# One mask and a tie count in place of sixteen strikes, with the next tile's maxima between dependent steps

## The reference

```python
q = (x @ Wq.T).reshape(b, n, 2, HEADS, DIM_KEY).transpose(2, 0, 1, 3, 4)
sim = jnp.einsum('pbnhd,hkpd->pbnhk', q, keys)
sx, ix = jax.lax.top_k(sim[0], 16)
sy, iy = jax.lax.top_k(sim[1], 16)
all_scores = (sx[..., :, None] + sy[..., None, :]).reshape(b, n, HEADS, 256)
scores, pk_indices = jax.lax.top_k(all_scores, 16)
h = gelu(einsum('bnd,bnhkd->bnhk', x, W_down[pk_indices]))
out = einsum('bnhk,bnhkd->bnd', h * softmax(scores), W_up[pk_indices])
```

## Time and profile before

| | us |
|---|---|
| median of 3 runs | 284.59 (283.16 to 284.63) |
| profiled execution | 284.64 |
| its span, first to last instruction | 282.8 |
| VectorE busy | 269.3 (95%) |
| TensorE busy | 242.3 (86%) |
| ScalarE busy | 236.1 (83%) |
| GpSimd busy | 224.1 (79%) |

### The profile page before, as it was taken

One profiled execution on the slowest core, in us unless ns is written; L12 is line 12 of the kernel. 1 busy time (PEld: TensorE's weight loads), 2 busy tenths in 40 slices (PEclk: granted clock), 3 DMA queues, 4 the chain that ended last, 5 costly groups with the idle time before them and its releaser, 6 DMA issues.

```text
span 282.8 us, 7961 instructions
## 1 busy us (share of the span) xinstructions
PE 242.3 (86%) x1574; PEld 176.7 (62%) x1574; DVE 269.3 (95%) x2580; ACT 236.1 (83%) x1047; POOL 224.1 (79%) x342
## 2 busy tenths in 40 slices
PE   7899797887988798989898889888888888889991
PEld 7566243575866675766576657666666666667780
DVE  5799999979999999999999999999999999999885
ACT  2465768589898999899989999999999999996943
POOL 7888610388688879997999799988998899888852
PEclk9999999797999999999999999999999999999997
DMA  7920000000000000100010001000010001000102
GB/s 174 279 71 2 0 1 0 2 1 0 5 1 0 5 0 3 39 1 3 1 38 3 1 0 38 7 0 5 10 31 2 0 1 41 2 1 3 37 3 74
DMA packets 11235, 6.29 MB, mean 22 GB/s; under 512 B 1457, under 2 KB 10674, under 8 KB 11186
## 3 DMA queue, kind: packets, MB, share of 16 engines
q1 hardware_dynamic: 9858, 5.12, 6.8%
q10 hardware_dynamic: 1328, 0.66, 1.1%
HBM read 3.67 MB, written 2.10 MB: 20 GB/s over the span
## 4 chain that ended last, share of the span: by engine, by line
DVE 62%; PE 14%; issue 8%; POOL 7%; ACT 6%; DMA 2%; ACTq 0%; POOLq 0%; DVEq 0%
DVE rest L1141 24%; DVE top L1130 13%; DVE top L1150 13%; DVE last L1174 6%; PE s_bank L1493 2%; DMA fwq_sb<-in_L_ffn_Wq 2%; POOL squareT L493 2%; DVE slot_gap L1159 2%; PE sim L1507 2%; PE f_bank L1500 1%; PE t_bank L1456 1%; PE c_bank L1500 1%; PE scratch L1487 1%; PE t_bank L1525 1%; POOL wgt L506 1%
## 5 line engine op out<-in xcount | busy, mean ns | idle before, releaser
L1141 DVE MATCH_REPLACE8 rest<-top,sim 128x32 f32<-128x32 f32 x512 | 85.8, 179 | 0.1
L1150 DVE MAX8 top<-rest 128x8 f32<-128x32 f32 x512 | 53.5, 177 | 0.7
L821 ACT ACTIVATE prob<-drop 128x50 f32<-128x50 f32 x224 | 51.6, 256 | 0.0
L1130 DVE MAX8 top<-sim 128x8 f32<-128x32 f32 x496 | 50.9, 178 | 0.6 <-PE sim L1507 0.6
L821 ACT ACTIVATION_READ_ACCUMULATOR prob<-drop 128x1 f32 x224 | 47.1, 214 | 0.0
L493 POOL TENSOR_TENSOR squareT<-sideT 100x512 bf16<-100x512 bf16 x31 | 32.5, 1048 | 15.2 <-ACT sideT L735 15.2
L1141 DVE MATCH_VALUE_LOAD rest<-top,sim 128x8 f32 x512 | 40.8, 80 | 0.3
L478 POOL TENSOR_TENSOR past<-gap,last 128x400 f32<-128x400 f32 x31 | 26.8, 864 | 11.2 <-DVE last L1174 11.2
L1507 PE MATMUL sim<-sim_w,xT_all 128*128 128x512 f32 x64 | 34.5, 621 | 0.8 <-ACT xT_all L771 0.8
L506 POOL TENSOR_TENSOR wgt<-prob,rden 128x400 f32<-128x400 f32 x30 | 25.6, 855 | 8.2 <-DVE rden L1120 8.2
L500 POOL TENSOR_TENSOR drop<-gap,out_by 128x400 f32<-128x400 f32 x30 | 31.0, 1034 | 0.9 <-ACT out_by L724 0.9
(11 more groups left out here) (289 smaller groups left out, 724.0 us busy)
## 6 DMA issues: line engine op xcount, KB each, us to landing
out<-y_sb SPq DMA_DIRECT2D x7, 256.0 KB, 2.3
x_sb<-in_L_attn_hidden_states SPq DMA_DIRECT2D x2, 256.0 KB, 4.0
fwq_sb<-in_L_ffn_Wq ACTq DMA_DIRECT2D x2, 256.0 KB, 6.0
x_sb<-in_L_attn_hidden_states SPq DMA_DIRECT2D x1, 512.0 KB, 5.4
wc_sb<-in_L_attn_Wc SPq DMA_DIRECT2D x1, 256.0 KB
out<-last_y SPq DMA_DIRECT2D x2, 128.0 KB, 1.9
wo_in<-in_L_attn_Wo SPq DMA_DIRECT2D x1, 192.0 KB
keys_sb<-in_L_ffn_keys ACTq DMA_DIRECT2D x1, 128.0 KB, 3.4
```

What stands on the lines that cost most here:

```text
L821: last = nc.scalar.activation(prob[d][:, h, :], drop[:, h, :], ACT.Exp, scale=-1.0, accum_out=den[d][:, h:h + 1])
L1130: last = nc.vector.max(top[d][:, v, 0:8], sim_bank[d][:, bass.ts(v, KEYS)])
L1141: last = nc.vector.match_replace(out=rest[:, v, :], in_to_replace=top[d][:, v, 0:8], in_values=sim_bank[d][:, bass.ts(v, KEYS)], imm_value ...
L1150: last = nc.vector.max(top[n % 2][:, v, 8:16], rest[:, v, :])
```

## The change

The strikes go. The eighth maximum of each vector becomes a threshold: one instruction marks all scores at or over it (`mark_above`, 16 x 32 elements, bf16 out), one adds the mark times -1e38 to the scores (`strike_above`). If scores equal to the eighth were struck too many, they have to come back: `sum_above` counts the marks of each vector into the freed bank, `spill_above` and `put_ties` turn a count over eight into copies of the eighth value in eight further columns of `rest` (now 40 wide), from which `next_8` takes its maxima. Each step needs the one before.

The order changes with it. In a turn, the `first_8` of the next tile stands in two halves between these steps, and the next tile's mark before `next_8`; `maxima` comes after `put_ties`. `top` has three buffers instead of two. `sim_used` is counted once a tile. TensorE computes the scores of tile n+2 late in turn n, not those of n+1 in the middle, and in the prelude the scores of tiles 2 to 5 stand earlier. The four `first_turn` calls are written out as `first_turns`, and the gaps of tile 1 are taken inside `select_tokens`. Lines of the same kind are left out where "..." stands.

```diff
+STRUCK = -1e38
+SPILL = 1e37
+TIES = VECS
-        top = [sb(f"top{i}", [P, VECS, TOPK]) for i in range(2)]
-        rest = sb("rest", [P, VECS, KEYS])
+        top = [sb(f"top{i}", [P, VECS, TOPK]) for i in range(3)]
+        above = sb("above", [P, VECS, KEYS], BF16)
+        rest = sb("rest", [P, VECS, KEYS + 8])
...
-            def strike_8(n, q):
...
-                for v in range(q * VECS // 4, (q + 1) * VECS // 4):
-                    last = nc.vector.match_replace(out=rest[:, v, :], in_to_replace=top[d][:, v, 0:8],
-                                                   in_values=sim_bank[d][:, bass.ts(v, KEYS)],
-                                                   imm_value=NO_SCORE)
+            def first_8(n, halves=range(2)):
+                if n >= 3:
+                    dve.wait_ge(topT_ready, n - 2)
+                dve.wait_ge(sim_ready, n + 1)
+                for v in range(HALF_V * halves[0], HALF_V * (halves[-1] + 1)):
+                    last = nc.vector.max(top[n % 3][:, v, 0:8], sim_bank[n % 2][:, bass.ts(v, KEYS)])
+                if 1 in halves:
+                    last.then_inc(sim_top8, 1)
+            def eighth(n, cols):
+                return top[n % 3][:, :, 7:8].to_broadcast([P, VECS, cols])
+            def mark_above(n):
+                dve.wait_ge(sim_top8, n + 1)
+                if n >= 1:
+                    dve.wait_ge(summed_above, n)
+                nc.vector.tensor_tensor(above[:, :, :], sim_bank[n % 2][:, :].rearrange("p (v k) -> p v k", k=KEYS),
+                                        eighth(n, KEYS), ALU.is_ge).then_inc(above_done, 1)
+            def strike_above(n):
+                dve.wait_ge(above_done, n + 1)
+                if n >= 1:
+                    dve.wait_ge(top_done, 2 * n)
+                nc.vector.scalar_tensor_tensor(rest[:, :, 0:KEYS], above[:, :, :], STRUCK,
+                                               sim_bank[n % 2][:, :].rearrange("p (v k) -> p v k", k=KEYS),
+                                               ALU.mult, ALU.add).then_inc(struck, 1)
+            def sum_above(n):
+                dve.wait_ge(struck, n + 1)
+                nc.vector.tensor_reduce(sim_bank[n % 2][:, 0:TIES], above[:, :, :], AX_X, ALU.add
+                                        ).then_inc(summed_above, 1)
+            def tie_slots(n):
+                return sim_bank[n % 2][:, TIES:TIES + 8 * VECS].rearrange("p (v k) -> p v k", v=VECS)
+            def spill_above(n):
+                dve.wait_ge(summed_above, n + 1)
+                nc.vector.scalar_tensor_tensor(tie_slots(n),
+                                               sim_bank[n % 2][:, 0:TIES].unsqueeze(2).to_broadcast([P, VECS, 8]), 2.0,
+                                               rank_row[:, 7:15].unsqueeze(1).to_broadcast([P, VECS, 8]),
+                                               ALU.mult, ALU.subtract).then_inc(spill_done, 1)
+            def put_ties(n):
+                dve.wait_ge(spill_done, n + 1)
+                nc.vector.scalar_tensor_tensor(rest[:, :, KEYS:KEYS + 8], tie_slots(n), SPILL, eighth(n, 8),
+                                               ALU.mult, ALU.min).then_inc(sim_used, 1)
...
             def select_tokens(n):
...
+                    if r == 2:
+                        gaps_of_pairs(n - 2)
+                        gaps_of_thirds(n - 2)
+                        last_gaps(n - 2)
...
+            def first_turns():
+                first_8(0)
+                dve.wait_ge(x_in[3], 16)
+                row_stats(4)
+                mark_above(0)
+                row_stats(5)
+                strike_above(0)
+                sum_above(0)
+                spill_above(0)
+                put_ties(0)
+                next_8(0, 0)
+                next_8(0, 1)
+                row_stats(6)
+                row_stats(7)
+                first_8(1)
...
+                next_8(2, 1)
+                select_tokens(3)
+                invert_gates()
+                mark_above(3)
+                strike_above(3)
+                first_8(4)
+                sum_above(3)
+                spill_above(3)
+                put_ties(3)
+                mark_above(4)
+                gaps_of_pairs(2)
+                next_8(3, 0)
+                gaps_of_thirds(2)
+                last_gaps(2)
+                next_8(3, 1)
+                invert_gate_sums()
             def turn(n):
                 b, j = divmod(n, TB)
+                strike_above(n)
+                if n + 1 in tiles:
+                    first_8(n + 1, [0])
+                sum_above(n)
+                invert_sums(n - 4)
+                spill_above(n)
+                if n + 1 in tiles:
+                    first_8(n + 1, [1])
+                put_ties(n)
                 if j == 0:
                     maxima(b - 1)
+                if n + 1 in tiles:
+                    mark_above(n + 1)
+                next_8(n, 0)
+                gaps_of_pairs(n - 1)
+                if j == 0:
                     inverse_row_sums(b - 1)
+                next_8(n, 1)
+                gaps_of_thirds(n - 1)
+                if n < TILES - 1:
                     last_gaps(n - 1)
...
             def scores(n):
                 pe.wait_ge(xt_out, n // TB + 1)
                 if n >= 2:
-                    pe.wait_ge(sim_used, 2 * n - 2)
+                    pe.wait_ge(sim_used, n - 1)
...
                     transpose_sides(n - 2)
                     pair_gaps(n - 1)
-                    scores(n + 1)
                     expert_weights(n - 4)
                     project_window(b, U_VW, wv_sb)
+                    if n + 2 in tiles:
+                        scores(n + 2)
                     count_places(n - 2)
...
                 if b == 4:
                     pe.wait_ge(gaps_of_done, 1)
                     pair_gaps(0)
-                    scores(2)
                     expert_parts()
                 if b + 2 < B:
                     transpose_rows(b + 2)
                 if b == 2:
+                    scores(2)
                     top_columns(0)
             product.then_inc(z_ready, 1)
+            scores(3)
             top_columns(1)
             pair_gaps(1)
-            scores(3)
...
             for b in range(B):
                 if b == 1:
                     transpose_gates()
+                if b == 4:
+                    scores(4)
                 hidden(b)
...
             count_places(0)
-            scores(4)
             transpose_masks()
             project_window(0, U_VW, wv_sb)
             count_ranks()
             transpose_sides(1)
+            scores(5)
             project_blocks(0)
```

More of the change, by code:

```diff
@@ L1147, in next_8 @@
+            def put_ties(n):
+                dve.wait_ge(spill_done, n + 1)
+                nc.vector.scalar_tensor_tensor(rest[:, :, KEYS:KEYS + 8], tie_slots(n), SPILL, eighth(n, 8),
+                                               ALU.mult, ALU.min).then_inc(sim_used, 1)
             def next_8(n, h):
-                dve.wait_ge(sim_used, 2 * n + 1 + h)
+                dve.wait_ge(sim_used, n + 1)
                 for v in range(h * HALF_V, (h + 1) * HALF_V):
-                    last = nc.vector.max(top[n % 2][:, v, 8:16], rest[:, v, :])
+                    last = nc.vector.max(top[n % 3][:, v, 8:16], rest[:, v, :])
@@ L1182, in select_tokens @@
             def select_tokens(n):
-                d = n % 2
+                d, top_n = n % 2, top[n % 3]
                 dve.wait_ge(sim_ready, n + 1)
-                dve.wait_ge(topT_ready, n - 1)
+                dve.wait_ge(topT_ready, n - 2)
                 dve.wait_ge(z_done, 1)
@@ L1230, in maxima @@
                                         negate=True).then_inc(max_done, 1)
[L1232 to L1251, removed]
-                    row_stats(6)
-                    row_stats(7)
-                if n == 2:
-                    select_tokens(3)
-                    invert_gates()
-                if n == 3:
-                    invert_gate_sums()
+            def first_turns():
[13 more added lines that the diff above has]
+                first_8(1)
+                mark_above(1)
+                strike_above(1)
+                first_8(2)
+                sum_above(1)
+                gaps_of_pairs(0)
+                spill_above(1)
+                put_ties(1)
+                mark_above(2)
+                next_8(1, 0)
+                gaps_of_thirds(0)
+                last_gaps(0)
+                next_8(1, 1)
+                strike_above(2)
+                sum_above(2)
+                spill_above(2)
+                put_ties(2)
+                next_8(2, 0)
+                next_8(2, 1)
[14 more added lines that the diff above has]
+                invert_gate_sums()
@@ L1314, in _ @@
-            for n in range(TB):
-                first_turn(n)
+            first_turns()
             for n in range(TB, TILES):
@@ L1517, in top_columns @@
                         t_bank[:, bass.ts(k, P)],
[L1518 removed]
```

(5 more changed lines are left out.)

73 lines of the change are left out of this document (7 added, 66 removed).

## The result

The changed kernel takes 290.25 us (median of four runs, 288.83 to 293.53), the kernel before 283.92 beside it. The ratio of 1.020 (95% interval 1.016 to 1.024) leaves out the run of 293.53, whose mean clock was lowest (0.960). Forecast were 286.7 and a loss of 2.1 us. The sign was right, the loss of 6.3 us by these medians three times that, and by the profiled executions twice. The profiled execution took 289.12 (span 287.4), 4.5 more than the profiled one of before.

The account below looks back on a forecast made before the run. VectorE sets the pace (28.75 of 28.87 us a batch), ScalarE 1.5 us behind. 284.64 plus 3.87 lost in the front minus 1.84 saved from turn 5 to turn 31 gives 286.7 us; range 279.5 to 291.

Parts of the forecast that it names:

- VectorE's prices: On VectorE, 0.60 us for each operation on 512 elements, 0.20 for each small one; turn 1 or 3 takes 6.65.
- rival A's second leg: On VectorE, a bf16 sum at twice the rate saves 0.27 a turn, about 7 us: 280; within a joint 0.17.
- Rival C: VectorE's new instructions cost their durations, not distances between starts: 2.61 instead of 2.20 a turn, about 296 us; chance 0.09.
- Turn 0: A batch's first turn: attention maxima at 3.27 instead of 2.42, VectorE's inverse waits for ScalarE's sums; 8.31 us, not 7.47.
- Turn 2: A batch's third turn: VectorE's pairs wait 0.37 for ScalarE's copy, 7.02 us; TensorE's scores of tile n+2 cost nothing.
- the 1.84 us: From tile 5's turn to tile 31's: 185.45 us instead of 187.29, so 1.84 saved.
- The front: Before turn 5: earlier scores on TensorE's path delay logits, gates and project_blocks; turn 5 at 71.0, 3.9 us lost.
- rival D: TensorE waits some 3 us for tile 5's scores, then runs at half clock: 2 us more on average, 288.7; chance 0.14.
- Rival B: The front's waits hide its scores, tile 5's don't hold project_blocks: turn 5 about 67, 282.8 to 283.5 us; chance 0.20.
- The tail: Past tile 31's turn, VectorE idles 0.92 us for ScalarE's copy; a shorter turn 31 alone buys nothing.
- Rival A: In steady batches, waits for ScalarE don't bind, VectorE's 27.42 us stands: 279.1; chance 0.17 together with a faster bf16 sum.

Follow-up runs that it names:

- experiment 3: Changed kernel with only the attention maxima of a batch's first tile moved from behind put_ties to behind invert_sums: 285.09 us, ratio 1.004.
- Experiment 7: Changed kernel with only turn 1's scores of tile n+2 moved from behind the expert weights to ahead of project_window(U_QW): 288.48 us, ratio 1.012.
- experiment 1: Changed kernel with only tile 5's scores moved in TensorE's prelude, from ahead of project_blocks(0) to behind project_selected(0): 287.52 us, ratio 1.015.
- experiment 9: Changed kernel again, unedited: 291.45 us, ratio 1.026; with 16 idle TensorE products ahead of tile 5's scores (the filling): 289.38 us, ratio 1.022.

## Why the prediction was right in sign and wrong in size

**VectorE's prices: right.** 0.60 for the large operations, 0.20 for the small, 6.65 for a plain turn. The sum over bf16 has its successor 0.59 us later, not 0.33, so rival A's second leg fell. Rival C wanted 0.67 or more between the starts and fell too.

**Turn 0: right.** The maxima go late, the inverse waits: 8.31 forecast, 8.28 found; moving them back (experiment 3) takes 0.92 off.

**Turn 2: the step that failed.** The prediction looks at the scores of tile n+2 on TensorE in turn 2 only. They push ScalarE's next copy back by 0.25 us, "which lies within its 0.9 us of slack at the maxima. I cost it at nothing; were that slack gone, it would be 0.25 a batch." For turn 2's scores that held. ScalarE does have this slack in the changed kernel, 1.17 us of idle time before the exponentials at 154.12 and 0.99 before those of the next batch (182.97):

```profile
154.12 0.33 ACT L926 ACTIVATE p_win<-s_bank,nmax 128x80 f32<-128x80 f32 x1 [1.17 <-DVE nmax L1266]
```

But the same scores stand in turn 1 too, and there the prediction has no term for them. They are ahead of attention_out on a TensorE without a gap, and they delay ScalarE between the exponentials and its copy in turn 2. The slack at the maxima lies behind that copy and can't help it, and the copy had no lead left: the paragraph before had it 0.37 late. Turn 2 came out 0.26 longer than forecast, and from turn 5 to turn 31 only 0.07 of the 1.84 us were saved. Experiment 7 moves turn 1's scores alone, leaves turn 2's, and finds the forecast's own 7.02. This step is 1.8 of the 2.5 us by which the profiled executions missed. That the "0.25 a batch" is so near to the measured 0.26 is luck: it was meant for other scores.

**The front: right in its mechanism, short by 0.6.** Logits and the gates' add-one moved by 1.2 and 1.9 (forecast 1.2 and 2.1), the put of tile 3 ended at 57.5 (57.7), and scores of tile 5 held project_blocks, as experiment 1 shows. Turn 5 came 4.48 late for 3.87: these scores ran at half clock and took 1.84 in place of 0.86, and the way from their end to turn 5 came out 0.3 shorter than forecast. That is rival D, with 0.14 given to it; all three profiles of this front in experiment 9 without the filling show it, and it costs 0.9 to 2.6 us. Rival B fell, since turn 5 came at 71.58 and not at 67. The step from the profiled execution to the median adds to the miss. The changed kernel's median is 1.1 above its profiled execution (mean clocks 0.992 in that, and 0.992, 0.977 and 0.960 in the others), while that of before is 0.7 below its own, which had a mean clock of 0.982 and two stretches at half clock.

**The tail: 0.2 more** than the nothing that it was given.

**Rival A** fell for the reason given against it. But it hid the useful statement: the same operations with the maxima early, the prelude's scores in their old places and turn 1's scores where TensorE waits give 277.3, faster than either kernel.

## What to carry to other kernels

Price a moved instruction in every turn in which it moves, and not in one for all. Slack takes up a delay only where it lies between the delay and the one who waits: here it lay behind the copy that was late. When the busiest engine is only a few per cent ahead of the next, take what a second engine waits for (here the maxima for the exponentials) out of the fast engine's queue first, and the fillers after it. And put work that moves on a full engine where that engine waits, not where its inputs happen to be ready.

## What the runs showed of the hardware

In and after one idle time of 3.7 us TensorE's clock stood at half for 3.4, 6.8 or 10.2 us in three executions with the same front; sixteen idle products in its place kept it at 1.0. The kernel before has a spread too: its 34 runs beside the experiments took 283.2 to 284.2 us at mean clocks of 0.988 to 0.998, and 284.4 to 285.8 at 0.980 to 0.986. project_blocks shows no trace of the clock: from its start to the next group it takes 1.83 at half clock (kernel of experiment 7) and 1.80 at full (the filled one). A reduction of 512 bf16 elements from SBUF has its successor 0.59 us later, no less than an operation on 512 elements of f32 (0.60).
